# One transformer layer on one core: the order of low rows and DMA transposes, the Exp table and evictions on ScalarE, and the last steps' second FFN product

## The reference

```python
x = L0_attn_x                                   # (4, 256, 256)
xn = _layernorm(x, axis=-1)
x = x + _L0_attn_ref(xn, Wq, Wkv_down, Wk_up, Wv_up, Wo) + _L0_ffn_ref(xn, w_fc, w_proj)
...
q = (x @ Wq.T).reshape(B, T, H, hd).transpose(0, 2, 1, 3)
latent = x @ Wkv_down.T                         # 64 channels, k and v come from it
att = softmax(where(mask, q @ k.T / 4, -inf))   # mask: last 64 columns, and the first 4
y = att @ v; return y @ Wo.T
...
def bitlinear(x, w):
    xn = layer_norm(x)
    x_hat = xn + jax.lax.stop_gradient(absmax_quant(xn) - xn)
    w_hat = w + jax.lax.stop_gradient(ternarize_weights(w) - w)
    return jnp.einsum('bsd,od->bso', x_hat, w_hat)
h = bitlinear(x, w_fc)                          # 256 -> 1024
h = jax.nn.gelu(h, approximate=False)
return bitlinear(h, w_proj)                     # 1024 -> 256
```

## Time and profile before

| | us |
|---|---|
| time, median of 3 runs | 153.37 |
| lowest and highest of them | 152.3, 153.66 |
| the profiled execution's own time | 153.69 |
| its span in the profile | 151.9 |
| TensorE busy in the span | 125.8 (83%) |
| VectorE busy | 101.9 (67%) |
| ScalarE busy | 82.7 (54%) |
| GpSimd busy | 32.5 (21%) |

### The profile page before, as it was taken

One profiled execution on the slowest core, in us unless ns is written; L12 is line 12 of the kernel. 1 busy time (PEld: TensorE's weight loads), 2 busy tenths in 40 slices (PEclk: granted clock), 3 DMA queues, 4 the chain that ended last, 5 costly groups with the idle time before them and its releaser, 6 DMA issues.

```text
span 151.9 us, 4970 instructions
## 1 busy us (share of the span) xinstructions
PE 125.8 (83%) x2156; PEld 92.8 (61%) x2156; DVE 101.9 (67%) x188; ACT 82.7 (54%) x124; POOL 32.5 (21%) x65
## 2 busy tenths in 40 slices
PE   7777897920899989995999899949999898967692
PEld 7566556820677646783776467836864457846581
DVE  0569899868329993479389934940699706983692
ACT  3599696750251557946415579542262769934110
POOL 8760600046000000064540000031500000027400
PEclk9999999996599999999999999995999999999998
DMA  4998500282733004268240030680400112935932
GB/s 130 302 320 303 155 11 0 76 155 52 143 54 91 4 0 78 65 127 102 52 143 6 0 69 4 125 87 0 132 11 6 36 37 43 161 76 107 117 129 69
DMA packets 32353, 13.59 MB, mean 89 GB/s; under 512 B 26948, under 2 KB 31976, under 8 KB 32232
## 3 DMA queue, kind: packets, MB, share of 16 engines
q1 hardware_dynamic: 30892, 11.90, 38.7%
q10 hardware_dynamic: 1440, 1.38, 3.1%
HBM read 6.19 MB, written 1.05 MB: 48 GB/s over the span
## 4 chain that ended last, share of the span: by engine, by line
PE 33%; DVE 26%; DMA 13%; SPq 10%; issue 8%; ACT 7%; POOL 1%; ACTq 0%; DVEq 0%
DMA gloT<-glo 9%; DVE mx L781 8%; PE ring L1093 6%; DVE rden L820 5%; PE acc L1169 4%; PE acc L1196 4%; DVE glo L814 3%; SPq L285 3%; SPq L291 3%; DMA wvu_r<-in_L_attn_Wv_up 3%; PE ring L1040 2%; PE ring L1169 2%; PE ring L1025 2%; PE acc L1188 2%; SPq L293 2%
## 5 line engine op out<-in xcount | busy, mean ns | idle before, releaser
L781 DVE TENSOR_REDUCE mx<-ring 128x8 f32<-128x1024 f32 x16 | 19.2, 1217 | 0.5 <-PE ring L1084 0.4
L503 ACT ACTIVATE E<-ring,un 128x1024 f32<-128x1024 f32 x16 | 17.0, 1112 | 1.9 <-PE ring L1138 1.3
L1169 PE MATMUL acc<-prT,ghT 128*128 128x256 f16 x48 | 11.5, 283 | 5.8 <-DMA gloT<-glo 5.8
L534 ACT ACTIVATE yhT<-y 128x256 f16<-128x256 f32 x8 | 3.3, 410 | 17.0 <-DVE y L825 17.0
L1025 PE MATMUL ring<-xhT,wqT 128*128 128x256 f16 x64 | 11.0, 287 | 1.5 <-DVE wqT L648 0.8
L814 DVE SCALAR_TENSOR_TENSOR glo<-gl,gam_r,gh 128x1024 f16<-128x1024 f32 x8 | 10.2, 1284 | 3.1 <-ACT gh L490 3.0
L1169 PE MATMUL acc<-prT,gloT 128*128 128x256 f16 x48 | 11.5, 284 | 0.0
L373 POOL TENSOR_SCALAR veh<-mvh 128x2 f32<-128x2 f32 x4 | 1.2, 308 | 47.8 <-DVE mvh L808 47.7
L474 ACT ACTIVATE gl<-ring,a 128x1024 f32<-128x1024 f32 x8 | 8.9, 1114 | 3.7 <-PE ring L1093 3.7
L1093 PE MATMUL ring<-fcT,xhT 128*128 128x512 f16 x32 | 9.5, 380 | 1.4 <-DVE mx L781 1.4
L347 POOL TENSOR_SCALAR ve<-mv 128x2 f32<-128x2 f32 x4 | 1.8, 456 | 40.0 <-DVE mv L717 40.0
(11 more groups left out here) (209 smaller groups left out, 369.6 us busy)
## 6 DMA issues: line engine op xcount, KB each, us to landing
wfc_r<-in_L_ffn_w_fc SPq DMA_DIRECT2D x1, 1024.0 KB, 7.5
wpr_r<-in_L_ffn_w_proj SPq DMA_DIRECT2D x1, 1024.0 KB, 8.9
xres<-in_L_attn_x SPq DMA_DIRECT2D x4, 256.0 KB, 2.8
bias<-in_c_bias SPq DMA_DIRECT2D x1, 825.0 KB
xin<-in_L_attn_x ACTq DMA_DIRECT2D x3, 256.0 KB, 3.4
out<-ob SPq DMA_DIRECT2D x3, 256.0 KB, 3.2
xin<-in_L_attn_x SPq DMA_DIRECT2D x1, 256.0 KB, 3.5
wq_r<-in_L_attn_Wq ACTq DMA_DIRECT2D x1, 256.0 KB, 4.0
```

The lines of the kernel that those rows point to most:

```text
L503: nc.scalar.activation(E[:, 2 * gp:2 * gp + 2, 2 * tp:2 * tp + 2, :].rearrange("p g t q -> p g (t q)"), slot("p2", b, r)[:], ACT.Exp, scal ...
L781: nc.vector.tensor_reduce(out=mx[:, i, 8 * gp:8 * gp + 8], in_=slot("f_p1", f, r)[:].rearrange("p a (t k) -> p (a t) k", t=NT), axis=AX.X, ...
L1169: last = nc.tensor.matmul(o.rearrange("p (c n) -> p c n", n=P), src[:, i, k, :], prT[:, :, k, :], start=((i == 0 or b == B - 1) and k == 0 ...
```

## The change

Its edits fall into five groups:

1. **Low rows and their transposes.** In step 0 `rows_high(1)` comes before the exponentials on ScalarE, and `rows_low(1)` before `first_ternary` on VectorE. SyncE issues batch 1's rows first and the ternary weight after them. The rows of a batch are turned by two transposes of 128x512 (high, low) in place of four of 128x256, and `xhT`, `xlT` have another layout for it (tile, channel block, row).
2. **Hidden layer.** ScalarE makes `hidden_high(b, 1)` right behind `hidden(b, 1)`, before the Exp table. VectorE makes `hidden_low(a, 0)` before `latents_low`, `hidden_low(a, 1)` before the statistics of the coming rows, and `hidden_stats(a, 0)` before `row_norm`. SyncE issues both high halves, then both low halves (steps 1 to 3, for batch a).
3. **Evictions.** `attended(b)` goes from the end of step b to the next step, behind its first two exponentials. `values(b, 0)` waits for it there.
4. **Maxima.** On VectorE `maxima(f, 2)` comes before `attended_low(b, 0)`.
5. **Last steps.** Batch 2's second product goes into a ring buffer, both tiles ahead of the last window scores; `values(3, 0)` no longer waits for its eviction. On ScalarE `hidden_high(3, 1)` comes before `ffn_scaled(2, ..)`.

The diff, cut to its core:

```diff
@@ ORDER
-                ORDER += score_slots(b, range(4)) + (projection_slots(f) if f < B else [])
+                ORDER += score_slots(b, range(3)) + ([("F2", a, 0, [(ffn_ok, a, TT_)])] if f == B else []) + score_slots(b, (3,))
+                ORDER += projection_slots(f) if f < B else []
@@ SyncE
-                    for i in range(TT_):
-                        sp.dma_start_transpose(dst[:, n % 3, :, i * P:(i + 1) * P], src[:, i, :]).then_inc(xT_ok[0], 16)
+                    sp.dma_start_transpose(dst[:, n % 3].rearrange("p i c n -> p (i c) n"), flat(src)).then_inc(xT_ok[0], 16)
...
                 if b:
-                    hidden_turned(b - 1, 0)
-                    hidden_turned(b - 1, 1)
+                    hidden_high_turned(b - 1, 0)
+                    hidden_high_turned(b - 1, 1)
+                    hidden_low_turned(b - 1, 0)
+                    hidden_low_turned(b - 1, 1)
                 else:
+                    rows_turned(1)
                     first_turned()
-                    rows_turned(1)
                     second_turned()
@@ ScalarE
+                if b == 0:
+                    rows_high(1)
                 sink_exponentials(b)
                 exponentials(b, 0)
-                if b == 0:
-                    rows_high(1)
                 exponentials(b, 1)
+                if b:
+                    attended(a)
...
                     hidden(b, 1)
+                    hidden_high(b, 1)
                     if f == B - 1:
                         hidden(f, 0)
                         hidden(f, 1)
                     table_ahead(b, ACT.Exp)
-                    attended(b)
-                    hidden_high(b, 1)
@@ VectorE
+                    hidden_low(a, 0)
                     if f < B:
                         latents_low(f)
-                    hidden_low(a, 0)
+                    hidden_low(a, 1)
                     if b + 2 < B:
                         row_stats(b + 2)
-                    hidden_low(a, 1)
+                    hidden_stats(a, 0)
                     if b + 2 < B:
                         row_norm(b + 2)
-                    hidden_stats(a, 0)
...
                     weight_means(0)
+                    rows_low(1)
                     first_ternary()
-                    rows_low(1)
...
+                    maxima(f, 2)
                     attended_low(b, 0)
-                    maxima(f, 2)
@@ TensorE
-                    wait(pe, ffn_ok, b - 1)
+                    wait(pe, att_ok, b - 1)
+                    wait(pe, ffn_ok, min(b - 1, B - 3))
...
                     window_scores(b, 2)
                     if b:
-                        second_product(a, 0, acc[:, 0:C])
+                        bank = take("F2", a)
+                        for i in range(TT_):
+                            second_product(a, i, bank[:, i, 0:C])
                     window_scores(b, 3)
-                    if b:
-                        second_product(a, 1, acc[:, C:2 * C])
```

40 lines of the change are left out of this document (22 added, 18 removed).

## The result

The changed kernel takes 141.19 us in the median of 4 runs (140.54 to 141.99), the kernel before, on the same chip, 153.51 (152.3 to 154.25). The ratio is 0.921, with a 95% interval of 0.913 to 0.928. A second set of runs of the unchanged new kernel gave 140.96 and 0.919 (0.912 to 0.926). The forecast was 139.6, with 137.2 to 143.0: the time lies inside, 1.6 above. The medians here are over all executions; the ratios leave out those that took over 1.5% more than the fastest of their kernel.

The account below looks back on a forecast made before the run. It took TensorE, busy 83%, to be bound by whatever feeds it late. Gains of 3.8 (step 0), 1.05 (maxima), 5.8, 0.7, 1.7 and 1.0 sum to 14.05, taking 153.69 to 139.6 us; range 137.2 to 143.0.

Parts of the forecast that it names:

- The hidden layer and the table: Steps 1 to 3: all five `gloT` waits go (5.8), two low-latents waits (0.7), and step 2's low clock (1.7).
- the rival of the new waits: Steps 1, 2: `a2`, query eviction or `gloT` ends waits, about 1 us each; tail loses 1.5; 141.5 to 143.4; chance 0.17.
- The 1.7 of step 2's clock: Step 2: its low clock follows a wait of 2.0 that goes, saving half of a 3.5 us stretch.
- GpSimd's `ve`: Hidden layer: beside one-input statistics `ve` escapes contention, `xn` some 0.9 earlier; `veh` now waits out `xl`'s 0.68; sum unchanged.
- Step 0 (3.8): Step 0: earlier low rows let `k_products` start 5.3 us earlier, bound by VectorE; less 1.5 for the clock: 3.8 gained.
- the clock behind the gap: Step 0: after TensorE's 3.2 us gap before `k_products` the clock falls, losing 1.5 us on `k_products` and `values(0, 0)`.
- Maxima (1.05): VectorE's `maxima(f, 2)` no longer waits for `attended_low(b, 0)`: TensorE's wait falls 0.35 in each of three steps, 1.05.
- Step 3 (1.42 + 1.0, and "one of the two stays"): Step 3: waits for `gloT` (1.42) and `ffn` (1.0) go; "issue" (1.44) or a last `gloT` wait (up to 1.5) stays.
- The tail (nothing counted): From the last output product to the end: no gain or loss forecast, 0.
- The clock holds and issue shrinks: Rival: no lower clock behind step 0's gap, and step 3's "issue" shrinks; 138.1, down to 137.0; chance 0.18.
- Step 0 does not do what it says: Rival: batch 1's merged transposes land as late as before relative to their issue queue; 143.4; chance 0.05.
- Slower: Rival: after step 0's gap the clock stays low through steps 0 and 1, worth 14 us: 154; chance 0.01.

Follow-up runs that it names:

- the filled gap: Changed kernel with four 512-wide products (16 instructions more) that compute nothing used, in step 0's gap before `k_products`: 139.25 us, ratio 0.903.
- the fill with 20 short products: Changed kernel with 20 one-tile float32 products (80 instructions more) in step 0's gap before `k_products`: 143.6 us, four executions from 139.65 to 145.48.

## Why the prediction was right, point by point

**The hidden layer and the table (5.8 + 0.7 + 1.7).** Right in the mechanism and in the sum: steps 1 and 2, with the maxima in them, gave 7.85 against 7.48 in the first pair of profiles, 7.06 in the mean of two pairs. `gloT` ends no wait, `a2` was ready at 69.0, 0.2 before the product's end at 69.2. So the rival of the new waits was near, but did not come. The 1.7 of step 2's clock must be read with care. That stretch was in one profile of the kernel before and not in the other; it was no debt of this wait alone. In the second profile the low clock cost more in step 0 instead (5.07 us of work at a clock of 0.50 from 39.8 to 44.9, against 3.46 at 0.52 from 38.5 to 42.0 in the first). With two profiles of each kernel the steps average as follows (starts of `xn` and of the output products; before 25.58 and 26.88, after 26.39 and 27.35):

| part, mean of two profiles | before | after | gain | forecast |
|---|---|---|---|---|
| start of `xn` | 26.23 | 26.87 | -0.64 | 0 |
| from there to step 0's output product | 32.78 | 29.29 | 3.49 | 4.15 |
| step 1 | 30.31 | 27.30 | 3.01 | 2.82 |
| step 2 | 34.77 | 30.72 | 4.05 | 4.66 |
| step 3 | 23.64 | 20.51 | 3.13 | 2.42 |
| tail | 4.38 | 5.08 | -0.70 | 0 |

The gains add up to 12.3, the forecast to 14.05. What is missing is the prologue (0.64), the tail (0.70), step 0 (0.66) and step 2 (0.61); the surplus of step 3 (0.71) and of step 1 (0.19) hides a part of it. That the time came within 1.6 owes that much to luck.

**GpSimd's `ve`.** The row of the changed kernel has 0.22, beside a statistics instruction with one input, where the earlier trace rows has 1.16 beside `glo` with two. With group 2 undone it takes 1.16 again, beside `glo` again. And `veh` takes 0.58 beside `xl`, which has two inputs:

```profile
63.65 0.22 POOL L352 TENSOR_SCALAR ve<-mv 128x2 f32<-128x2 f32 x1 [25.97 <-DVE mv L725]
...
67.25 0.58 POOL L378 TENSOR_SCALAR veh<-mvh 128x2 f32<-128x2 f32 x1 [0.93 <-DVE mvh L816]
```

The trace agrees with the rule that the Trainium skill gives (SBUF — State Buffer, "Who interferes with whom"): the `ve` part and the `veh` part both went as it says, and `xn`, which had waited 0.91 for the row scale that GpSimd makes from `ve`, now has no wait. One reading of the forecast was wrong: `veh` does not come to stand beside `xl` only now, it took 0.58 beside `xl` in the kernel before too.

**Step 0 (3.8).** The order of events was right: no wait before the latents, one gap in front of `k_products`, ended by `latS`, the lower clock behind it. Two sizes were off. `latS` ended at 39.25, not at 38.1: 0.81 of that is the prologue, and the rest is `xl`: it started at 28.72, 0.5 after `xh`'s end at 28.21, where the forecast had it follow at once, and VectorE, idle for 0.83 where it had been for 0.45, passed the delay on to both ternary weights. And **the least certain term is the clock behind the gap**: "I take 1.5 of it as lost". The stretch lasted 6.8 us in the profiled run and 3.4 in the next, which costs 3.0 and 1.6. Of six profiles with this gap four have the short one, and the filled gap puts the price at 1.7 to 1.9 in the median. So the 1.5 was a little small as a rule and half of the price in some executions. The forecast had taken one stretch of 3.5 as the measure, without a spread.

**Maxima (1.05).** Right; 1.3 us of waits come back when the order is undone, and steps 1 and 2 grow by about 0.3 and 0.45.

**Step 3 (1.42 + 1.0, and "one of the two stays").** The 2.42 are there, and 1.0 more (0.7 in the mean of two profiles): "issue" went from 1.44 to 0.62, and the last `gloT` was in time (issued at 129.13, landed 3.4 later at 132.5, needed at 132.9). The forecast had counted one of the two as staying. How close it was the variants show: "issue" is 0.57 to 1.10 in them, and the last `gloT` ends a wait of 0.2 to 0.3 in four. What the engine does in "issue" no run shows.

**The tail (nothing counted).** This is the step that was missing. The text said of the last product's `gloT` what would be late next, but followed only TensorE. Behind it stand two transfers of batch 2's end: the load of `xres`, which must wait until GpSimd has used the old rows, and the store of `ob`. The load is bound twice: GpSimd's sum over the old rows ends at 130.24, and SyncE comes to the load at 130.73, right behind its issue of the last `gloT`. It then lands 4.1 later, the store 5.2. Against the kernel with the last edit undone they got no earlier, while TensorE's last step got 2.2 to 2.5 us shorter. As a rule it is `xres` that ends the wait (six of eight profiles), not the store. The term is 0.8 us in their mean, 0.2 to 1.4 each; it takes back a part of group 5.

**The rivals.** "The clock holds and issue shrinks" was half true: the clock did not hold, "issue" shrank. "New waits" came, but in the tail and not at `a2`. "Step 0 does not do what it says" was wrong: `xlT` landed 2.5 after its issue. "Slower" never was near.

## What to carry to other kernels

When a gap on the bound engine is shortened and not closed, part of its price stays: here 7.08 us became 3.6 to 3.7, and the clock fell in either case. Order and merging together gave 3.5 us in step 0 (the maxima's 0.35 in it); closing the rest (the low latents first) gave 2.3 to 2.5 more, filling it with a few wide products that compute nothing 1.7 to 1.9. And two edits that shorten the same wait do not add up: each alone gave most of it.

When the last steps get faster, follow the loads and stores of the step before the last to the very end. A buffer that served all steps became the bound of the last one; with two small tiles of their own the last sums follow TensorE again, worth 0.2 to 1.4 us from execution to execution.

A clock stretch read in one profile is one draw. Profile both kernels twice before a term rests on where it lies. And compare by steps: they repeat to 0.1 us where whole times scatter by 1 to 2.

## What the runs showed of the hardware that was not expected

- The same gap of 3.5 to 3.7 us was followed by 3.4 us at 1.2 GHz in four profiled executions and by 6.8 in two. A wait of 1.95 to 2.0 was followed by the lower clock in one of three profiles, one of 1.83 (the fill with 20 short products) and one of 2.30 (four transposes) too, one of 1.86 and one of 2.51 (group 2 undone, step 3) not. The length of the gap alone doesn't decide. What else does, these runs leave open.
- A transposing DMA of `gloT` lands in 3.0 to 3.4 us, or in 4.2 to 5.0. Of the slow ones looked at, each has an instruction load in its stretch of the transfer view: in the kernel before, between 67 and 72 us

```profile
q8 instruction: 1, 0.02, 1.3%
...
gloT<-glo SPq DMA_TRANSPOSE x1, 4.3
```

  and in the fill with 20 short products between 115 and 121 (above). The reverse does not hold: the fill with few instructions has such a load in the stretch of its step 3 transposes too, and 3.2. That the load is the cause is a reading of these coincidences, not shown. Nor is it shown that adding instructions moves step 3: one execution of the fill with 80 took 139.65, about as long as the fill with 16 (139.25).
- Merging transposes of 128x256 into ones of 128x512 changed for the low rows neither the issue (1.25 and 1.27 in the median) nor the landing (2.4 and 2.5) of one instruction. For the high rows it changed both a little (issue 1.25 and 1.8, landing 2.6 and 3.1 in the median). For batch 1's rows SyncE issues for 2.6 us instead of about 5.
